# An xDeepFM forward pass on one core: rows laid out through DRAM, eight of thirteen row pairs copied by DMA, layer 1 in plain fp32

## The chip, the core and the metric

The kernel runs on one core of one Trainium2 chip. The metric is the device time of one execution in microseconds. The engines are TensorE (PE), VectorE (DVE), ScalarE (ACT), GpSimd (POOL) and SyncE (SP, which only issues DMAs here).

## The reference

512 samples with 26 sparse features each; every feature has a table of 1250 rows of 32 numbers, and 13 dense inputs stand beside them. What costs time:

```
emb = tables[feat_idx, sparse]                     # 512 x 26 x 32
x0 = xk = emb
for w, bb in ((conv1_w, conv1_b), (conv2_w, conv2_b)):          # the two CIN layers
    hp = einsum('bhd,bmd->bhmd', xk, x0).reshape(-1, h * M, E)  # all products of rows
    xn = sigmoid(einsum('oi,bid->bod', w, hp) + bb[None, :, None])   # 128 outputs
    xk = xn[:, :64];  res.append(xn[:, 64:])
cin_out = concatenate(res, axis=1).sum(-1) @ cin_w + cin_b
h1 = tanh([emb, dense] @ W1 + b1); h2 = tanh(h1 @ W2 + b2); h3 = tanh(h2 @ W3 + b3)   # 845-1024-512-256
out = linear + cin_out + h3 @ deep_w + deep_b + bias
```

Layer 1 has 26 x 26 products (351 different ones, as it is symmetric), layer 2 has 64 x 26. Only the second half of layer 2's outputs is needed.

## The kernel before, in words

**Tiling.** The batch is cut into 16 pairs of 32 samples (`NPAIR`), a pair into two halves c of 16 samples. Half a pair is 16 x 32 = 512 columns (`CH`), so a tile of both halves is 128 partitions by 1024 columns.

**Rows.** For each pair POOL gathers the table rows (`gather`, L287 to L299: 7 indirect DMAs) into `emb`, with the sample in the partition. SP then lays them out (`lay_out`, L252; `lay_out_half`, L230 to L239) with 10 small SBUF to SBUF DMAs into `raw`: the feature in the partition, 26 of them in partitions 0 to 25 for c = 0 and 64 to 89 for c = 1, and (sample, element) in the columns. ACT rounds `raw` into `x` (`x_high`, L489) and DVE writes the rest, raw minus rounded, 32 partitions further down (`x_low`, L595), so that a selection matrix over 58 partitions rebuilds full fp32 in one fp32r matmul.

**Layer 1.** `sums_of` (L358) lets PE add row pairs by a selection matrix, in three tiles u of 117 pairs. ACT squares them twice (L508 and L509: plain and rounded), POOL (DVE for the first ones) takes the difference `sq_lo`. `layer1` (L369) makes nine fp32r matmuls per half: high weights by high squares, low by high, high by low, for three u. ACT's `sigmoid` (L511) then makes `xk` (64 rows, written twice, to partitions 0 and 64) and `res1`.

**Layer 2.** Thirteen tiles t (`T2`): tile t pairs `xk` with features 2t and 2t+1. `spread_tile` (L384) broadcasts these two feature rows over 64 partitions each, by matmul into a PSUM ring of three slots, DVE multiplies them by `xk` into `prod` (L668), and `main` (L396) makes four fp32 matmul records per tile, 128 x 64 for each half, into `conv`. The sums tiles share the three ring slots with the spread tiles (`enter`, `freed_by`).

**Order.** Each engine has its program written out by hand. PE works in groups of two tiles (`GROUPS`, seven groups): first the spread tiles of the next group, then the sums of a later pair where `SUMS_IN` says so, then `main` of this group's tiles, then half a layer 1 of the next pair where `L1_IN` says so. In DVE's order of products, `X_LOW_AT`, `TURN_AT` and `FOLD1_AT` say after which tile t the other work comes. ACT's order per pair i (L554 to L568) is `sigmoid2(i-1)`, the squares of pair i+1, `x_high(i+2)`, the sigmoids of i+1, and squares of i+2. SP's order is `lay_out(i+3)` and the load of one weight piece.

**Deep part.** W1, W2, W3 are loaded in pieces and split by POOL into high and low parts (`split_piece`, L311). Behind the last pair PE runs the three deep layers at three fp32r matmuls per product (L463).

Of the kernel before, what the change touches and what calls it, by code (L numbers as in the profile page):

```python
# [5 lines left out]
F32 = mybir.dt.float32  # L6
# [28 lines left out]
WP = 1024  # L35
DENSE_AT = 96
RX = 3
SQR = 4
GSEM = 4
RING = 3  # L40
RP = 4
SUMS_IN = ({1: (1, 0), 2: (1, 1), 3: (1, 2)},
# [3 lines left out]
L1_IN = ({4: 0, 5: 1}, {3: 0, 4: 1}, {2: 0, 3: 1}, {2: 0, 3: 1})  # L46
X_LOW_AT, TURN_AT, FOLD1_AT, LOW_AT = (12, 11, 7, 7), (9, 9, 9, 9), (5, 5, 7, 7), 7
WARM = 60
PIECE_AT = 8
# [4 lines left out]
W1A_AT = IND_AT + 3 * PB  # L54
# [6 lines left out]
def build(nc, idx, table, dense_t, const, w2, mlp1, mlp2, mlp3, sel2, out):  # L61
    with ExitStack() as ctx:
# [23 lines left out]
        ind_sb = const_sb[:, IND_AT:W1A_AT].rearrange("p (k b) -> p k b", b=PB)  # L86
# [5 lines left out]
        lin = sb("lin", [P, NPAIR, 2])  # L92
# [87 lines left out]
        def piece(k):  # L180

            if k < K1:
                n = P if k < K1 - 1 else K1_LAST
                return (wpiece[k % 2][0:n, :], mlp1[k * P:k * P + n, :], m1_hi[0:n, k, :], m1_lo[0:n, k, :])
            if k < PIECES - 1:
                j = 2 * (k - K1)
                return (wpiece[k % 2][:, :].rearrange("p (k n) -> p k n", k=2),
                        mlp2[j * P:(j + 2) * P, :].rearrange("(k p) n -> p k n", p=P),
                        m2_hi[:, j:j + 2, :], m2_lo[:, j:j + 2, :])
            return (wpiece[k % 2][:, :].rearrange("p (k n) -> p k n", k=K3),  # L190
                    mlp3.rearrange("(k p) n -> p k n", p=P), m3_hi[:, :, :], m3_lo[:, :, :])

        GROUPS = [(2 * g, 2 * g + 1) for g in range(T2 // 2)] + [(T2 - 1,)]
        slot_of, freed_by = {}, {}

        def sums_in(i, g):

            ahead, u = SUMS_IN[min(i, 3)].get(g, (0, 0))
            return (i + ahead, u) if ahead and i + ahead < NPAIR else None
# [9 lines left out]
        for t in GROUPS[0]:  # L209
            enter(("spread", t))  # L210
        for i in range(NPAIR):
            for g in range(len(GROUPS)):
                ahead = [T2 * i + t for t in GROUPS[g + 1]] if g + 1 < len(GROUPS) else \
                    [T2 * (i + 1) + t for t in GROUPS[0]]
                for r in ahead:
                    if r < NTILE:
                        enter(("spread", r))
                if sums_in(i, g):
                    enter(("sums",) + sums_in(i, g))
# [9 lines left out]

        def lay_out_half(eng, i, c):  # L230

            s, at = i % RX, HALF * c
            for g in range(NG):
                eng.dma_start(raw[s][at + g * GM:at + (g + 1) * GM, :], emb[:, i, 1 + NG * c + g, 0:E])\  # L234
                   .then_inc(raw_in[s], 16)
            for q in range(ML):
                n = q * 2 * CB + c * CB
                eng.dma_start(raw[s][at + NG * GM + q:at + NG * GM + q + 1, :],  # L238
                              emb[n:n + CB, i, 0, 0:E]).then_inc(raw_in[s], 16)  # L239
# [5 lines left out]
        def _(sp):  # L245
# [6 lines left out]
            def lay_out(i):  # L252

                s = i % RX
# [5 lines left out]
                for c in range(2 if i else 1):  # L260
                    lay_out_half(sp, i, c)
# [5 lines left out]
            for i in range(RX):  # L267
                lay_out(i)
# [3 lines left out]
            for i in range(NPAIR):  # L272
                if i + RX < NPAIR:
                    lay_out(i + RX)
                if 0 <= i - PIECE_AT + 2 < K1:
                    load_piece(i - PIECE_AT + 2)
            for k in range(K1, PIECES):
                load_piece(k)
# [522 lines left out]
```

## Time and profile before

| | us |
|---|---|
| time of the runs | 473.8 median of 3 (472.45 to 473.81) |
| the profiled execution's own time | 473.61 |
| its span | 471.8, at a mean granted clock of 0.978 |
| pairs 0 to 15 end | at 67.0 (pair 0) to 398.5 (pair 15) |
| deep layers and the end | 398.9 to 471.8 |

Busy, of the span: PE 94%, DVE 68%, POOL 58%, ACT 42%. DMA moved 12.04 MB, 26 GB/s in the mean. The busy share of an engine says how much it works, not whether it sets the end: that is read in the chain of waits. The clock is the one that TensorE was granted, 1.00 being 2.4 GHz and 0.50 being 1.2 GHz.

### The profile page before, as it was taken

What the parts mean: (1) busy time and instruction counts of PE and PEld (TensorE: products, weight loads), DVE (VectorE), ACT (ScalarE), POOL (GpSimd) and SP (SyncE); (2) the same over time, 40 slices, a digit from 0 to 9 for tenths busy, and PEclk for the clock granted to TensorE, in tenths of its full rate; (3) what the DMA queues carried; (4) which work ended last, traced back from release to release, by engine and by line L of the source; (5) the groups of instructions that cost most, each with busy time, mean ns of one, the idle gap of its engine ahead of it and who ended that gap; (6) DMA issues with size and microseconds to landing.
All of it is one profiled execution on the core that took longest, in us unless ns stands there. A gap on an engine that the chain in (4) does not pass through costs nothing.

```text
span 471.8 us, 5582 instructions
## 1 busy us (share of the span) xinstructions
PE 443.0 (94%) x2006; PEld 209.7 (44%) x2006; DVE 322.3 (68%) x351; ACT 199.7 (42%) x346; POOL 273.4 (58%) x238
## 2 busy tenths in 40 slices
PE   3574989999999999999999999999999999999998
PEld 3541334343434342434333434334343423888685
DVE  4137757787787888787969797978798687442111
ACT  3063354736464645546363635353546340111111
POOL 6343658685747566666687869686854444930000
PEclk9858899999999999999999999999999999999999
DMA  5100100100000000011102121202110100300000
GB/s 180 14 13 10 15 15 13 15 10 12 9 11 11 10 10 10 11 54 14 51 13 52 15 52 17 50 15 51 26 60 0 46 0 1 124 9 2 0 1 0
DMA packets 21945, 12.04 MB, mean 26 GB/s; under 512 B 17206, under 2 KB 19638, under 8 KB 21918
## 3 DMA queue, kind: packets, MB, share of 16 engines
q1 hardware_dynamic: 17862, 9.87, 7.7%
q0 software_dynamic: 3584, 1.76, 3.2%
q8 instruction: 16, 0.26, 0.2%
q10 hardware_dynamic: 472, 0.05, 0.1%
q14 instruction: 11, 0.09, 0.1%
HBM read 9.96 MB, written 0.00 MB: 21 GB/s over the span
## 4 chain that ended last, share of the span: by engine, by line
PE 77%; DVE 8%; issue 7%; POOL 3%; DMA 3%; SPq 1%; ACTq 1%; ACT 0%; DVEq 0%
PE conv L402 34%; PE conv L380 15%; PE ring L392 10%; DVE prod L668 8%; PE conv L463 7%; PE ring L463 7%; PE ring L365 3%; POOL emb L296 3%; DMA raw<-emb 1%; DMA emb<-in_table,rows 1%; SPq L234 1%; ACTq L234 1%; DMA idx_sb<-in_idx 0%; PE conv L482 0%; SPq L238 0%
## 5 line engine op out<-in xcount | busy, mean ns | idle before, releaser
L668 DVE TENSOR_TENSOR prod<-ring,xk 128x1024 f32<-128x1024 f32 x208 | 242.7, 1217 | 72.2 <-PE ring L392 65.7
L402 PE MATMUL conv<-prod,w_sb 128*64 128x512 f32 x832 | 205.1, 611 | 0.1
L308 POOL TENSOR_TENSOR sq_lo<-sq,sq_hi 117x512 fp32r<-117x512 f32 x88 | 110.5, 1288 | 71.1 <-ACT sq_hi L509 67.9
L296 POOL DMA_INDIRECT emb<-in_table,rows x112 | 110.3, 985 | 52.5 <-issue 29.4
L402 PEld LDWEIGHTS conv<-prod,w_sb 128*64 128x64 f32 x832 | 49.8, 136 | 93.9 <-issue 82.6
L519 ACT ACTIVATE xk<-conv,const_sb 64x512 f32<-64x512 f32 x64 | 43.7, 683 | 107.1 <-PE conv L380 106.3
L392 PE MATMUL ring<-x,sel_sb 58*128 58x512 f32 x416 | 80.8, 456 | 6.2 <-DVE prod L668 3.6
L508 ACT ACTIVATE sq<-ring 117x512 f32<-117x512 f32 x96 | 58.9, 614 | 54.2 <-PE ring L365 53.9
L392 PEld LDWEIGHTS ring<-x,sel_sb 58*128 58x128 f32 x416 | 33.1, 186 | 85.6 <-issue 41.0
L509 ACT ACTIVATE sq_hi<-ring 117x512 fp32r<-117x512 f32 x96 | 59.5, 620 | 0.0
L380 PE MATMUL conv<-sq_hi,w_hi 117*128 117x512 f32 x96 | 42.2, 439 | 0.0
L380 PE MATMUL conv<-sq_hi,w_lo 117*128 117x512 f32 x96 | 38.9, 405 | 0.0
L380 PE MATMUL conv<-sq_lo,w_hi 117*128 117x512 f32 x96 | 38.5, 401 | 0.0
L600 DVE TENSOR_TENSOR x<-raw,x 26x512 fp32r<-26x512 f32 x32 | 23.9, 748 | 14.7 <-ACT x L496 13.8
L365 PE MATMUL ring<-x,sel_sb 58*117 58x512 f32 x96 | 21.3, 447 | 12.9 <-DVE prod L668 7.8
L380 PEld LDWEIGHTS conv<-sq_hi,w_hi 117*128 117x128 f32 x96 | 18.6, 194 | 28.0 <-issue 12.6
L316 POOL TENSOR_TENSOR m_lo<-wpiece,m_hi 128x1024 fp32r<-128x1024 f32 (+1 forms) x12 | 29.8, 2487 | 1.0
L521 ACT ACTIVATE res<-conv,const_sb 64x512 f32<-64x512 f32 x32 | 21.9, 684 | 0.8
L699 DVE CAST h_hi<-hf 128x512 fp32r<-128x512 f32 x8 | 5.6, 705 | 24.3 <-ACT hf L588 24.3
L529 ACT ACTIVATE res<-conv,const_sb 128x512 f32<-128x512 f32 x16 | 11.0, 689 | 26.2 <-PE conv L402 26.2
L380 PEld LDWEIGHTS conv<-sq_lo,w_hi 117*128 117x128 f32 x96 | 18.6, 194 | 4.5
L380 PEld LDWEIGHTS conv<-sq_hi,w_lo 117*128 117x128 f32 x96 | 18.6, 194 | 3.0
(78 smaller groups left out, 307.1 us busy)
## 6 DMA issues: line engine op xcount, KB each, us to landing
wpiece<-in_mlp SPq DMA_DIRECT2D x11, 512.0 KB, 3.6
emb<-in_table,rows POOLq DMA_INDIRECT x112, 2.4
raw<-emb SPq DMA_DIRECT2D x93, 16.0 KB
raw<-emb SPq DMA_DIRECT2D x62, 2.0 KB
sel_f<-in_sel SPq DMA_DIRECT2D x1, 832.0 KB, 6.1
const_sb<-in_const SPq DMA_DIRECT2D x1, 658.0 KB, 4.5
w_sb<-in_w SPq DMA_DIRECT2D x1, 416.0 KB, 6.6
wpiece<-in_mlp SPq DMA_DIRECT2D x1, 308.0 KB
```

The costliest lines, as they stand in the source:

```text
L296: pool.indirect_dma_start(out=emb[0:n, i, j, :], out_offset=None, in_=table, in_offset=bass.IndirectOffsetOnAxis(ap=rows[0:n, i, j:j + 1], ...
L308: nc.gpsimd.tensor_tensor(sq_lo[0:UK, u, c, :], sq[0:UK, s % SQR, :], sq_hi[0:UK, u, c, :].bitcast(F32), ALU.subtract).then_inc(lo_done, 1)
L316: nc.gpsimd.tensor_tensor(lo, src, hi.bitcast(F32), ALU.subtract).then_inc(piece_lo, 1)
L365: mm = nc.tensor.matmul(sums_bank(i, u)[0:UK, c, :], sel1_sb[at:at + XK, u, :], x[i % RX][at:at + XK, :], start=True, stop=True)
L380: mm = nc.tensor.matmul(l1_bank(i, c)[:, :], w[:, u, :], s[0:UK, u, c, :], start=(u == 0 and k == 0), stop=(u == UT - 1 and k == 2))
L392: mm = nc.tensor.matmul(spread_bank(r)[:, c, :], sel2_sb[at:at + XK, t, :], x[i % RX][at:at + XK, :], start=True, stop=True)
L402: mm = nc.tensor.matmul(conv[i % 2][c * HALF:(c + 1) * HALF, :], w2_sb[:, t, :], prod[r % RP][:, c, :], start=(t == 0), stop=(t == T2 - 1))
L463: mm = nc.tensor.matmul(MLP_BANKS[n % 2], w[0:r, k, mt * P:(mt + 1) * P], h[0:r, k, :], start=(k == 0 and j == 0), stop=(k == kt - 1 and j ...
L508: nc.scalar.activation(sq[0:UK, s % SQR, :], sums_bank(i, u)[0:UK, c, :], ACT.Square)
L509: nc.scalar.activation(sq_hi[0:UK, u, c, :], sums_bank(i, u)[0:UK, c, :], ACT.Square).then_inc(hi_done, 1)
L519: nc.scalar.activation(xk[i % 2][q * HALF:(q + 1) * HALF, c, :], bank[0:HALF, :], ACT.Sigmoid, bias=small_sb[0:HALF, C_CB1:C_CB1 + 1]).the ...
L668: nc.vector.tensor_tensor(prod[r % RP][:, :, :].rearrange("p c n -> p (c n)"), spread_bank(r)[:, :, :].rearrange("p c n -> p (c n)"), xk[i ...
```

## The change

What it does:

- **Rows.** The gathers take 4 indirect DMAs per pair instead of 7. SP writes the gathered rows into a DRAM buffer `laid` (26 rows of 1024 numbers per pair, 2 DMAs in `lay_out`), and reads them back into `raw` with 2 DMAs (`fetch`).
- **Copies.** For 8 of the 13 tiles (`COPIED`) the broadcast by matmul falls away. SP reads `laid` with `copy`: two DMAs per tile, each of one 4 KB row of DRAM into 64 partitions, into a ring of `RC` = 5 tiles. DVE multiplies such a tile by `xk` in place, and `main` reads it there. Five tiles (0, 1, 5, 6, 10) go through PSUM as before, with `prod` cut to 3.
- **Groups.** PE works in three groups, (0 to 4), (5 to 9), (10 to 12); `SUMS_IN`, `L1_IN`, `X_LOW_AT`, `FOLD1_AT` are new.
- **Layer 1 in plain fp32.** One square per tile and half, no difference, three fp32 matmuls per half instead of nine fp32r ones.
- **Weight pieces.** Half as large (512 columns), 24 instead of 12. The 14 of W1 are split by ACT (`piece_high`) and DVE (`piece_low`) in pairs 1 to 14; POOL keeps the last ten behind the pairs. During the pairs POOL only gathers.

```diff
-RP = 4
-SUMS_IN = ({1: (1, 0), 2: (1, 1), 3: (1, 2)},
...
-X_LOW_AT, TURN_AT, FOLD1_AT, LOW_AT = (12, 11, 7, 7), (9, 9, 9, 9), (5, 5, 7, 7), 7
+RP = 3
+COPIED = (2, 3, 4, 7, 8, 9, 11, 12)
+SPREAD = tuple(t for t in range(T2) if t not in COPIED)
+NC, NS = len(COPIED), len(SPREAD)
+RC = 5
+LAY_AT = 3
+GROUPS = ((0, 1, 2, 3, 4), (5, 6, 7, 8, 9), (10, 11, 12))
+SUMS_IN = ({1: ((1, 0), (1, 1)), 2: ((1, 2),)},
+           {0: ((1, 0),), 1: ((1, 1), (1, 2)), 2: ((2, 0),)},
+           {0: ((1, 1),), 1: ((1, 2), (2, 0)), 2: ((2, 1),)},
+           {0: ((1, 2),), 1: ((2, 0),), 2: ((2, 1),)})
+L1_IN = ({2: (0, 1)}, {1: (0,), 2: (1,)}, {1: (0,), 2: (1,)}, {0: (0,), 1: (1,)})
+X_LOW_AT, TURN_AT, FOLD1_AT, PIECE_AT = (12, 11, 4, 3), (9, 9, 9, 9), (5, 5, 7, 7), 11
...
             def lay_out(i):
                 sp.wait_ge(rows_in[i % GSEM], ROWS * (i // GSEM + 1))
+                sp.dma_start(laid[i, 0:NG * GM, :].rearrange("(j m) (b e) -> (m b) j e", m=GM, e=E),
+                             emb[:, i, 0:NG, 0:E]).then_inc(laid_in[i % RX], 16)
+                sp.dma_start(laid[i, NG * GM:M, :].rearrange("m (b e) -> (m b) e", e=E),
+                             emb[0:ML * PB, i, NG, 0:E]).then_inc(laid_in[i % RX], 16)
+            def fetch(i):
+                sp.wait_ge(laid_in[i % RX], LAID * (i // RX + 1))
                 if i < RX:
                     sp.wait_ge(raw_zero, i + 1)
                 else:
                     sp.wait_ge(x_lo_done, 2 * (i - RX + 1))
+                for c in range(2):
+                    sp.dma_start(raw[i % RX][HALF * c:HALF * c + M, :], laid[i, :, c * CH:(c + 1) * CH])\
+                      .then_inc(raw_in[i % RX], 16)
+            def copy(n):
+                r = tile_of_copy(n)
+                i, t = r // T2, r % T2
+                if n >= RC:
+                    sp.wait_ge(main_done, tile_of_copy(n - RC) + 1)
+                sp.wait_ge(laid_in[i % RX], LAID * (i // RX + 1))
+                for k in range(2):
+                    sp.dma_start(copied[n % RC][HALF * k:HALF * (k + 1), :, :].rearrange("p c n -> p (c n)"),
+                                 laid[i, 2 * t + k, :].partition_broadcast(HALF)).then_inc(copy_in[n % RC], 16)
...
             for i in range(NPAIR):
+                if i < KW:
+                    load_piece(i)
+                for k in range(NC):
+                    n = NC * i + RC + k
+                    if n < NC * NPAIR:
+                        copy(n)
+                    if i == 0 and k == 1:
+                        lay_out(2)
+                        fetch(2)
+                    if k == (NC - 1 if i < 2 else LAY_AT) and i + RX < NPAIR:
+                        lay_out(i + RX)
                 if i + RX < NPAIR:
+                    fetch(i + RX)
...
                 for u in range(UT):
+                    pe.wait_ge(sq_done, 2 * (UT * i + u) + c + 1)
+                    mm = nc.tensor.matmul(l1_bank(i, c)[:, :], w1_sb[:, u, :], sq[i % 2][0:UK, u, c, :],
+                                          start=(u == 0), stop=(u == UT - 1))
...
+                    if t in COPIED:
+                        dve.wait_ge(copy_in[n % RC], 32 * (n // RC + 1))
+                        left = copied[n % RC]
+                    else:
+                        dve.wait_ge(spread_done, n + 1)
+                        if n >= RP:
+                            dve.wait_ge(main_done, tile_of_spread(n - RP) + 1)
+                        left = spread_bank(r)
```

## Rows read from the trace of the kernel before

**Rows 1.** The page's first part: busy us, share of the span, instructions

```profile
PE 443.0 (94%) x2006; PEld 209.7 (44%) x2006; DVE 322.3 (68%) x351; ACT 199.7 (42%) x346; POOL 273.4 (58%) x238
```

**Rows 2.** Groups by line: busy us, mean ns of one, then idle before and releasers

```profile
L668 DVE TENSOR_TENSOR prod<-ring,xk 128x1024 f32<-128x1024 f32 x208 | 242.7, 1217 | 72.2 <-PE ring L392 65.7 <-ACT xk L519 6.4
```

**Rows 3.** Windows, one pair: length, busy per engine, clock, DMA share, GB/s

```profile
249.17:271.60 22.43, 22.16 (x104) 8.87 (x102) 18.16 (x20) 11.38 (x20) 17.73 (x16) 1.00 0.17 34
```

**Rows 4.** Chain of waits in that pair: start, us, what (a few pieces)

```profile
254.59 1.87 PE conv L402 x8
...
261.27 2.30 PE conv L380 x9
263.57 0.66 PE ring L392 x4
264.23 0.23 PE ring L365 x2
```

**Rows 5.** Timeline at the end: a plain fp32 matmul, four records of 512 columns

```profile
467.62 1.88 PE L482 MATMUL conv<-h,const_sb 128*1 128x512 f32 x4
```

**Rows 6.** Timeline of ACT: sigmoid of layer 2, ends of pairs 3, 13 and 15

```profile
135.95 0.69 ACT L529 ACTIVATE res<-conv,const_sb 128x512 f32<-128x512 f32 x1 [0.81 <-PE conv L402]
...
360.31 0.69 ACT L529 ACTIVATE res<-conv,const_sb 128x512 f32<-128x512 f32 x1 [0.81 <-PE conv L402]
...
398.51 0.69 ACT L529 ACTIVATE res<-conv,const_sb 128x512 f32<-128x512 f32 x1 [11.93 <-PE conv L402]
```

**Rows 7.** Chain of waits in the first 46 us (the fourth gather, last landing, layout)

```profile
9.16 0.95 POOL emb L296
...
12.91 2.33 DMA emb<-in_table,rows
...
18.49 1.83 DMA raw<-emb
```

**Rows 8.** Timeline of ACT and DVE, first pair

```profile
20.35 0.63 ACT L496 ACTIVATE x<-raw 96x512 fp32r<-96x512 f32 x1 [10.98 <-DMA raw<-emb]
23.34 0.60 ACT L508 ACTIVATE sq<-ring 117x512 f32<-117x512 f32 x1 [2.36 <-PE ring L365]
23.83 0.59 ACT L509 ACTIVATE sq_hi<-ring 117x512 fp32r<-117x512 f32 x1
...
35.00 1.39 ACT L519 ACTIVATE xk<-conv,const_sb 64x512 f32<-64x512 f32 x2 [0.45 <-PE conv L380]
...
36.49 3.49 DVE L668 TENSOR_TENSOR prod<-ring,xk 128x1024 f32<-128x1024 f32 x3 [6.44 <-ACT xk L519]
```

**Rows 9.** Bulk DMA: an issue, landing of pieces, windows (length, clock, DMA share, GB/s)

```profile
227.86 0.58 SPq L250 DMA_DIRECT2D wpiece<-in_mlp  x1
...
DMA to landing us min/median/max: 3.5/3.6/4.5
...
341.00:343.00 2.00, 1.00 0.42 152
229.00:231.00 2.00, 1.00 0.76 260
3.00:7.00 4.00, 1.00 1.00 394
```

**Rows 10.** Windows of PE (busy, granted clock, DMA share, GB/s) and its timeline

```profile
40.90:43.60 2.70, 0.00 (x0) 1.00 0.04 3
43.60:50.20 6.60, 5.62 (x16) 0.50 0.12 13
...
44.58 0.78 PE L365 MATMUL ring<-x,sel_sb 58*117 58x512 f32 x2 [3.80 <-DVE prod L668]
```

**Rows 11.** One tile's instructions (min, median, max ns), and timeline of POOL in pair 15

```profile
L600 DVE TENSOR_TENSOR x<-raw,x x32: 681/682/2776, 21.0 to 347.2; 26x512 fp32r<-26x512 f32 x32
...
383.54 8.80 POOL L338 TENSOR_TENSOR xt_lo<-xt,xt_hi 128x512 fp32r<-128x512 f32 x7 [12.14 <-ACT xt_hi L576]
```

More of the change, by code:

```diff
@@ L58, with build @@
 CONST = SEL1_AT + NPR
-def build(nc, idx, table, dense_t, const, w2, mlp1, mlp2, mlp3, sel2, out):
+def build(nc, idx, table, dense_t, const, w2, mlp1, mlp2, mlp3, sel2, laid, out):
     with ExitStack() as ctx:
@@ L180, in piece @@
         def piece(k):
[L182 to L189, printed above, removed]
@@ L199, in sums_in, with spreads_in, spreads_up_to @@
-            return (i + ahead, u) if ahead and i + ahead < NPAIR else None
+            return [(i + ahead, u) for ahead, u in SUMS_IN[min(i, 3)].get(g, ()) if i + ahead < NPAIR]
+        def spreads_in(i, g):
+            if g + 1 < len(GROUPS):
+                return [T2 * i + t for t in GROUPS[g + 1] if t in SPREAD]
+            return [T2 * (i + 1) + t for t in GROUPS[0] if t in SPREAD and i + 1 < NPAIR]
+        def spreads_up_to(r):
+            return NS * (r // T2) + SPREAD.index(r % T2) + 1
@@ L208, in build @@
             enter(("sums", 0, u))
-        for t in GROUPS[0]:
-            enter(("spread", t))
+        for r in spreads_in(-1, len(GROUPS) - 1):
+            enter(("spread", r))
         for i in range(NPAIR):
             for g in range(len(GROUPS)):
[L213 to L219, printed above, removed]
+                for r in spreads_in(i, g):
+                    enter(("spread", r))
+                for j, u in sums_in(i, g):
+                    enter(("sums", j, u))
         def l1_bank(i, c):
@@ L266, in _ @@
             sp.dma_start(w2_sb[:, :, :], w2).then_inc(w2_in, 16)
-            for i in range(RX):
-                lay_out(i)
+            lay_out(0)
+            fetch(0)
+            for n in range(RC):
+                copy(n)
+            lay_out(1)
+            fetch(1)
             sp.wait_ge(zeroed, 1)
@@ L320, in _ @@
             pool.wait_ge(idx_step, 5)
-            for i in range(RX):
+            for i in range(NPAIR):
                 gather(i)
-            for i in range(NPAIR):
-                if i + 1 < NPAIR:
-                    for u in range((1, 0, 1)[i] if i < 3 else 2, UT):
-                        low(i + 1, u)
-                if i + RX < NPAIR:
-                    gather(i + RX)
-                if 0 <= i - PIECE_AT < K1:
-                    split_piece(i - PIECE_AT)
-                if i and i + 2 < NPAIR:
-                    for u in range(1 if i == 1 else 2):
-                        low(i + 2, u)
             for k in range(K1):
@@ L341, in _ @@
             pool.wait_ge(lin_done, 1)
-            for k in range(K1, PIECES):
+            for k in range(KW, PIECES):
                 split_piece(k)
@@ L530, in sigmoid2, with piece_high @@
                                      bias=small_sb[:, C_CB2:C_CB2 + 1]).then_inc(l2_read, 1)
+            def piece_high(k):
+                src, _, hi, _ = piece(k)
+                act.wait_ge(piece_in[k % 2], 16 * (k // 2 + 1))
+                nc.scalar.activation(hi, src, ACT.Copy).then_inc(piece_hi, 1)
             act.wait_ge(zeroed, 1)
@@ L558, in _ @@
                         squares(i + 1, u)
+                        if (i, u) == (2, 1):
+                            x_high(i + 2)
                 if i == 1:
                     sigmoid(2, 0)
-                if i + 2 < NPAIR:
+                if i != 2 and i + 2 < NPAIR:
                     x_high(i + 2)
+                if i <= KW:
+                    piece_high(i - 1)
                 if i + 1 < NPAIR:
@@ L565, in _ @@
                         sigmoid(i + 1, c)
+                        if (i, c) == (2, 0):
+                            squares(4, 0)
                 if i + 2 < NPAIR:
-                    for u in range(1 if i == 1 else 2):
+                    for u in range(1 if i == 2 else 0, 1 if i == 1 else 2):
                         squares(i + 2, u)
             act.wait_ge(l1_done, 2 * NPAIR)
-            act.wait_ge(lo_done, 2 * UT * NPAIR)
             act.wait_ge(turned, 2 * NPAIR)
@@ L796 @@
             for k, v in arrays.items()}
+    laid = nc.dram_tensor("laid", (NPAIR, M, 2 * CH), F32, kind="Internal").ap()
     out = nc.dram_tensor("out_row", (B,), F32, kind="ExternalOutput").ap()
-    build(nc, out=out, **args)
+    build(nc, laid=laid, out=out, **args)
     r = run_bass_kernel_spmd(nc, [{f"in_{k}": v for k, v in arrays.items()}], core_ids=[0])
```

207 lines of the change are left out of this document (82 added, 125 removed), and 3 rows, old and new, of the table SUMS_IN.

## The prediction

> **What bounds the kernel now.** I read the page's busy shares first: PE 94%, DVE 68%, POOL 58%, ACT 42% [rows 1]. That names a candidate. The window of one steady pair confirms it: 22.16 of 22.43 us are PE, at the full clock, while DVE has 18.16 [rows 3]. The chain of waits in that pair shows what fills it: two tiles of `main` take 1.87, half a layer 1 takes 2.30, two spread tiles with the change of matmul kind before and after 0.66, a sums tile 0.23 [rows 4]. So PE sets the pace, and a DVE product (1.217 alone [rows 2], 1.14 back to back, as three take 3.49 [rows 8]) waits 65.7 us in all for the ring. Pair 3 ends at about 135.75, pair 13 at 360.1, pair 15 at 398.35 (each sigmoid of layer 2 starts 0.2 behind) [rows 6]: 22.44 per pair in between. All sums below go by the profiled execution, 473.6, which stands 0.2 under the median of 473.8.
>
> **PE's work per pair.** Spread tiles: 8 of 13 go, and four of seven group changes. Per pair before, 13 x 0.935 + 2 x 2.30 + spreads and sums of some 5.7 = 22.4. After: `main` stays 12.15. Five spreads and three sums cost 8 x 0.23 + 3 x 0.2 for the changes = 2.4, that is 0.90, 0.66 and 0.90 in the three groups. Layer 1 does not get cheaper: a plain fp32 matmul of 512 columns is two records of about 0.43 each, since four take 1.88 less a tail of 0.17 [rows 5]; three per half are 6 x 0.43 to 0.45 = 2.65, against 2.30. PE's own floor is 12.15 + 5.3 + 2.4 = 19.9 per pair.
>
> **DVE.** 18.16 [rows 3] plus 0.7 for `piece_low` = 18.9. I take a product from SBUF at the price of one from PSUM; the row of x_low, an SBUF by SBUF operation of 512 columns at 682 ns [rows 11], would give 0.15 + 2 x 0.53 = 1.22, the same. ACT loses half its squares and gains 0.6 of `piece_high`; it is not near 19.9. The squares' difference on POOL hid beside PE and frees nothing on the path.
>
> **The loop through xk.** Layer 1's second half now ends in group 1, and the next pair's products wait for the sigmoids: 0.2 + 1.39 [rows 8] = 1.65; five products and x_low, 5.8 + 1.4 (two operations of 0.68 [rows 11]); `main` of tile 4, 0.93; first half 2.65; group change 0.66; `main` of 5 to 9, 4.67; second half 2.65. Sum 20.4. With nothing else in the way a pair would take 20.4, 2.0 less than now.
>
> **The loop through fetch, which I think decides.** In pair i (from 3 on) DVE does x_low(i+2) behind product 3. That needs x_high(i+2), which needs `raw`, fetched by SP at the end of its iteration i-1. In front of this fetch stands the copy of tile 8 of pair i, which waits for `main` of tile 12 of pair i-1: the end of that pair. Call this end zero.
> Issues: a bulk DMA takes SP 0.58, 0.63 with the step to the next [rows 9]. The copy of tile 7 (freed by tile 11) issues at -0.7, that of tile 8 at 0.5 to 1.8, the fetch at 1.8 and 2.4. The last small layout DMA landed 1.83 from its issue [rows 7], so 4.25 is the earliest with 0.58 issues. If an issue costs 0.43 it is 3.5.
> Transfer: the copies of tiles 7 and 8 are 1 MB in the same queue ahead of the fetch. No row shows a load into only 64 partitions. Bounds: the 128-partition loads ran at 394 GB/s when the queue was full, the one 77-partition piece at 152 against 260 for a full piece seen alone [rows 9]. 64 partitions are nearer to 77 than to 128, so there will be a loss; I take half of 394, 200 GB/s, or 1.31 per 256 KB transfer (0.66 and 1.7 at the ends). A piece's bytes moved from about 1.1 behind its issue and it landed 0.5 behind the last of them. So: first byte at 0.4, four transfers 5.25, the fetch's 0.1 MB 0.25, 0.5: `raw` lands at 6.4.
> The Trainium skill, page SBUF — State Buffer, section "Door 1: The DMA port swizzle", says that partitions 0 to 63 reach only 8 of 16 ports, 196 GB/s against 328 for 128 partitions at 1 MiB, and that two DMAs to the two halves gain only 6%. By it a copy takes 2.6 us. No run here shows it yet; it speaks against a change that sends 67 MB to SBUF in halves of 64 partitions.
> From there: x_high 0.05 + 0.64, x_low 0.05 + 1.40, product 4 1.20; then 0.93 + 2.65 + 0.66 + 4.67 + 2.65 + 0.90 + 2.80 (tiles 10 to 12) = 15.27. Period = landing + 18.6 = 25.0.
> Clock: PE stands still from 4.65 (`main` of tile 3) to 9.75, 5.1 us per pair. In the trace before, PE stood still for 3.8 us ahead of 44.58; the granted clock was 0.50, the 1.2 GHz level, from 43.6 to 50.2, with 5.62 us busy in it [rows 10], so work worth 2.8 was lost. I take 2.5. Period 27.5.
> Ten pairs (4 to 13): 10 x (27.5 - 22.44) = +50.6. With the ends of my bounds: landing 3.5 gives 22.1 (-3), 152 GB/s lands at 8.0 and gives 26.6 + 2.5 = 29.1 (+67).
>
> **The first pairs.** The fourth gather starts at 9.16 and would land 2.33 later, 11.5, instead of 15.24 for the seventh [rows 7]. Writing to `laid` (two issues and a landing of 2.3, bounds 1.8 and 3.5) and the fetch bring `raw` at 17.7 instead of 20.3. Six squares at 0.48 instead of twelve [rows 8] end at 23.7; the first half of layer 1 runs at the low clock (5.1), the second not (2.65), sigmoids 1.6: first product at 32.6 instead of 36.49 [rows 8]. Pair 0: 18.4 of DVE, `main` 0.9, then both halves of layer 1 uncovered and the sigmoids around x_high(2), 6.5 = 25.8. Pairs 1 and 2: DVE 19, `main` 0.9, half a layer 1 2.65, 1.65, stalls for x_low of 0.6 and 1.5: 24.8 and 25.7. Pair 3 meets its `raw` in time: 22.6. It ends at 131.5, against 135.75: -4.2 (bounds -8 and +1, as the clock may fall in the uncovered stretches).
>
> **The end.** Pair 14 has no x_low: 19.5. Pair 15 is DVE's 16.9 behind xk: 19. POOL's seven differences, 8.8 us in pair 15 [rows 11], now lie beside products with two SBUF operands; x_low, also such, once took 2776 ns instead of 682 beside POOL's work [rows 11]. I add 3 (0 to 7). 41.5 against 38.25: +3.3. The deep part keeps its matmuls: 0. What hides POOL's last ten pieces is the deep layer 1; each costs a load that lands in 3.6 [rows 9] and a split, shared by two buffers. Without that cover it would be up to 5.
>
> **Sum.** 473.6 - 4.2 + 50.6 + 3.3 = 523.
>
> **Rivals.**
> - *Half rate, clock kept.* Same loop, but PE is granted 1.00: period 25.0, 473.6 - 0.9 + 25.6 = 498. For it: the trace has one such fall in the pairs, and a standstill that comes in every pair may be met otherwise. Against it: 5.1 us is more than the 3.8 that was enough [rows 10]. 0.14.
> - *Full rate.* The copies move as fast as 128-partition loads; the issues decide, landing 3.5 to 4.25, period 22.1 to 22.9, 469 to 477; with an occasional fall of the clock up to 490. The busy engines of the 77-partition piece moved as much each as those of a full one (152 at a share of 0.42, 260 at 0.76 [rows 9]), which speaks for it. 0.22, of which a quarter is faster than before.
> - *The fetch is no bound (other side).* If `raw` lands within 1.8 us of the pair's end, or another order of events hides it, the xk loop sets the pace: 20.4, so 473.6 - 0.9 - 20.4 = 452. It decides below a landing of 1.8; the break-even of the whole is 3.9. For it: PE loses 2.5 us of work and ACT has slack. Against it: two waits and four issues in one queue. 0.22.
> - *The copies bind by volume.* 4.2 MB per pair at 152 GB/s are 27.6 us, to which the fetch, the layout, the gathers and a weight piece add over 1 us: 29 per pair, 473.6 - 0.9 + 66 = 539. The DMA engines would never rest. 0.10.
>
> **Chances.** The forecast has 0.32, the volume case 0.10, clock kept 0.14, full rate 0.22, fetch no bound 0.22. A change of 0.3% (1.4 us) is about what this kernel's times can tell. Faster: 0.22 + 0.06 = 0.28; same 0.04; slower 0.68. The range leaves out a tenth on each side: 454 to 542. The likeliest case's own range is 507 to 540.
>
> **What would show it.** Step by step in the changed profile: DVE's wait at x_low for ACT's x, some 4 us per pair, and ACT's x_high waiting for DMA raw; PE idle near 5 us per pair ahead of `main` of tile 4, with a clock of 0.5 behind it; half a layer 1 at 2.65; a copy's 256 KB transfers spaced 1.3 us; first product near 32.6; pair 3 ending near 131. Wrong: a DMA share near 1 only half the time with copies at 0.7 each (full rate), or pairs of 20 to 21 us with PE busy throughout (no bound).

## The result, and the profile after

| | before | after |
|---|---|---|
| median of the runs, us | 473.5 | 594.1 (591.4 to 598.2, 4 runs) |
| ratio | 1 | 1.2555 [1.2510, 1.2599] |
| span of the profiled execution | 471.8 | 596.3, mean granted clock 0.88 |

The kernel before ran at 473.5 beside it. Slower by 120.6 us where 49.5 were forecast: the right side, but outside the range of 454 to 542. The profiled execution of the changed kernel is the slowest of its four, 4 us above the median, so the rows below add up to 124.5 and not to 120.6. Of the kernel in "The first pairs again" four of six runs were over 1.5% longer than its fastest, and its time and ratio are those of the other two. The first part of the changed kernel's page, beside [rows 1], shows TensorE with more busy time although it has 354 fewer matmul records, and idle for a fifth of the span:

```profile
PE 462.9 (78%) x1652; PEld 186.8 (31%) x1652; DVE 317.8 (53%) x356; ACT 162.7 (27%) x264; POOL 151.0 (25%) x146
```

The sigmoid of layer 2 marks the ends of pairs 3, 13 and 15, as in [rows 6]:

```profile
162.58 0.69 ACT L550 ACTIVATE res<-conv,const_sb 128x512 f32<-128x512 f32 x1 [3.34 <-PE conv L430]
...
483.44 0.69 ACT L550 ACTIVATE res<-conv,const_sb 128x512 f32<-128x512 f32 x1 [3.34 <-PE conv L430]
...
522.44 0.69 ACT L550 ACTIVATE res<-conv,const_sb 128x512 f32<-128x512 f32 x1 [15.54 <-PE conv L430]
```

From these rows and the spans, term by term (us):

| stretch | before | after | moved | forecast |
|---|---|---|---|---|
| start to the end of pair 3 | 135.95 | 162.58 | +26.6 | -4.2 |
| pairs 4 to 13 | 224.36 | 320.86 | +96.5 | +50.6 |
| pairs 14 and 15 | 38.20 | 39.00 | +0.8 | +3.3 |
| deep layers, end | 73.3 | 73.9 | +0.6 | 0 |

A steady pair takes 32.09 instead of 22.44. The page's list of waits (us in total, times, longest) names the loop that was forecast, fetch to x_high to x_low to product to `main` of tile 4, and one wait that was not, that of the sums (L394) for ACT's squares:

```profile
DVE x L628 <- ACT x L520: 118.1, 14, 10.9
...
PE conv L430 <- DVE copied L694: 62.2, 15, 7.6
ACT x L520 <- DMA raw<-laid: 59.6, 12, 10.5
...
PE ring L394 <- ACT sq L529: 31.7, 12, 2.6
```

The chain of waits (start, us, what) through one steady pair, from the end of the pair before at 322.60 (`...` marks pieces left out):

```profile
318.16 4.44 PE conv L430 x12
322.60 0.02 issue
322.62 0.45 SPq L297
...
323.11 0.60 SPq L297
...
323.80 0.50 SPq L286
...
324.34 5.09 DMA raw<-laid
...
329.46 0.64 ACT x L520
...
330.83 0.68 DVE x L628
...
331.55 1.24 DVE copied L694
...
332.83 1.98 PE conv L430 x4
334.80 3.44 PE conv L408 x6
338.24 0.44 PE ring L420 x2
338.68 0.23 PE ring L394 x2
338.91 4.44 PE conv L430 x20
343.35 2.79 PE conv L408 x6
...
347.58 0.68 ACT res L542
...
348.29 1.09 ACT sq L529 x2
...
349.43 0.50 PE ring L394 x2
```

Read it downwards: the copy's issue waits for the pair's last `main`, and the fetch stands behind it in SyncE's queue. Beside this chain TensorE still has spreads, sums and `main` of tiles 0 to 3 to do, up to 327.06; then it stands for 5.77 us, as its timeline shows:

```profile
332.83 1.98 PE L430 MATMUL conv<-copied,w_sb 128*64 128x512 f32 x4 [5.77 <-DVE copied L694]
```

Behind it comes a cold stretch, one in which the granted clock has fallen (0.70 from 332.83 to 338.24): 1.98 for `main` of tile 4 and 3.44 for half a layer 1, against 1.08 and 2.79 where the clock is full. At 346.14 it leaves TensorE a second time, for ACT's sigmoids and squares, and comes back at 349.43; the twelve records behind that gap take 4.44, which is the first line (the same place one pair earlier); the granted clock is 0.64 from 349.9 to 354.4. The windows of that pair and of its copies (length, busy per engine, clock, DMA share, GB/s), beside [rows 3]:

```profile
322.60:354.30 31.70, 23.29 (x82) 7.56 (x82) 18.41 (x20) 9.21 (x15) 6.83 (x8) 0.84 0.65 151
322.60:329.30 6.70, 4.46 (x22) 1.45 (x22) 0.00 (x0) 1.78 (x3) 0.99 (x2) 1.00 1.03 233
```

While copies run the DMA engines are full (share 1.03) at 233 GB/s, not 394 as for 128 partitions in [rows 9]. Over the whole pair their share is 0.65, so volume does not bind.

### The profile page after: what moved, and what is told of

Its sections match the earlier page's. It is cut to its first block, busy times and chain, and to the rows that moved or that the text cites. A ratio compares the mean times of both kernels' runs of the same rounds, so it can differ in the third digit from the quotient of the medians.

```text
span 596.3 us, 4837 instructions
## 1 busy us (share of the span) xinstructions
PE 462.9 (78%) x1652; PEld 186.8 (31%) x1652; DVE 317.8 (53%) x356; ACT 162.7 (27%) x264; POOL 151.0 (25%) x146
## 4 chain that ended last, share of the span: by engine, by line
PE 58%; issue 10%; DMA 9%; DVE 9%; SPq 6%; ACT 6%; POOL 1%; DVEq 0%
PE conv L430 26%; PE conv L408 16%; DMA raw<-laid 8%; PE conv L487 6%; PE ring L487 5%; SPq L297 5%; DVE copied L694 5%; PE ring L420 2%; DVE prod L694 2%; PE ring L394 2%; ACT sq L529 2%; DVE x L628 2%; ACT xk L540 2%; ACT x L520 1%; ACT res L542 1%
## 5 line engine op out<-in xcount | busy, mean ns | idle before, releaser
L430 PE MATMUL conv<-copied,w_sb 128*64 128x512 f32 x512 | 146.5, 699 | 67.0 <-DVE copied L694 62.2
L694 DVE TENSOR_TENSOR copied<-copied,xk 128x1024 f32<-128x1024 f32 x128 | 156.2, 1244 | 10.6 <-DMA copied<-laid 10.2
L694 DVE TENSOR_TENSOR prod<-ring,xk 128x1024 f32<-128x1024 f32 x80 | 94.9, 1215 | 84.7 <-ACT xk L540 78.8
L408 PE MATMUL conv<-sq,w_sb 117*128 117x512 f32 x192 | 110.0, 718 | 2.2 <-ACT res L542 2.2
L430 PE MATMUL conv<-prod,w_sb 128*64 128x512 f32 x320 | 90.7, 683 | 0.7 <-DVE prod L694 0.7
L430 PEld LDWEIGHTS conv<-copied,w_sb 128*64 128x64 f32 x512 | 39.6, 156 | 159.3 <-DVE copied L694 84.1
L628 DVE TENSOR_TENSOR x<-raw,x 26x512 fp32r<-26x512 f32 x32 | 21.8, 682 | 118.7 <-ACT x L520 118.1
L408 PEld LDWEIGHTS conv<-sq,w_sb 117*128 117x128 f32 x192 | 41.4, 231 | 78.8 <-issue 75.4
L394 PE MATMUL ring<-x,sel_sb 58*117 58x512 f32 x96 | 21.2, 453 | 41.4 <-ACT sq L529 31.7
L420 PE MATMUL ring<-x,sel_sb 58*128 58x512 f32 x160 | 34.6, 483 | 12.7 <-DVE prod L694 8.9
L367 POOL TENSOR_TENSOR xt_lo<-xt,xt_hi 128x512 fp32r<-128x512 f32 (+1 forms) x7 | 15.4, 2248 | 83.5 <-ACT xt_hi L604 83.5
L430 PEld LDWEIGHTS conv<-prod,w_sb 128*64 128x64 f32 x320 | 20.1, 147 | 38.9 <-issue 34.6
L420 PEld LDWEIGHTS ring<-x,sel_sb 58*128 58x128 f32 x160 | 13.5, 192 | 56.1 <-issue 31.8
L520 ACT ACTIVATE x<-raw 96x512 fp32r<-96x512 f32 x16 | 10.1, 630 | 59.6 <-DMA raw<-laid 59.6
L394 PEld LDWEIGHTS ring<-x,sel_sb 58*117 58x117 f32 x96 | 9.1, 188 | 48.5 <-ACT sq L529 36.9
```

Source lines behind the costliest of these rows:

```text
L394: mm = nc.tensor.matmul(sums_bank(i, u)[0:UK, c, :], sel1_sb[at:at + XK, u, :], x[i % RX][at:at + XK, :], start=True, stop=True)
L408: mm = nc.tensor.matmul(l1_bank(i, c)[:, :], w1_sb[:, u, :], sq[i % 2][0:UK, u, c, :], start=(u == 0), stop=(u == UT - 1))
L420: mm = nc.tensor.matmul(spread_bank(r)[:, c, :], sel2_sb[at:at + XK, t, :], x[i % RX][at:at + XK, :], start=True, stop=True)
L430: mm = nc.tensor.matmul(conv[i % 2][c * HALF:(c + 1) * HALF, :], w2_sb[:, t, :], prod_of(r)[:, c, :], start=(t == 0), stop=(t == T2 - 1))
L628: nc.vector.tensor_tensor(x[i % RX][at + XLO:at + XK, :], raw[i % RX][at:at + M, :], x[i % RX][at:at + M, :].bitcast(F32), ALU.subtract).t ...
L694: nc.vector.tensor_tensor(prod_of(r)[:, :, :].rearrange("p c n -> p (c n)"), left[:, :, :].rearrange("p c n -> p (c n)"), xk[i % 2][:, :, ...
```

## The experiments

Each kernel is the changed one with the edit shown, unless it says otherwise. "Steady pair" is the mean of pairs 4 to 13. In the edits `...` marks lines left out, and copies are counted from 0. The kernel before took 471.4 to 472.9 beside them.

**The fetch moved forward.** Behind copy 5 instead of behind copy 7 of its pair.

```
+FETCH_AT = 5
...
-                if i + RX < NPAIR:
-                    fetch(i + RX)
+                    if k == (NC - 1 if i < 2 else FETCH_AT) and i + RX < NPAIR:
+                        fetch(i + RX)
```

> SP fetches raw(i+3) behind the copy that tile 9 frees instead of behind the one that tile 12 frees. Theory (each steady pair of 32.1 us is a loop through the late fetch, with a ring-slot wait of 3 and a fallen clock on top): DVE's wait for x_high, 118 us in all, falls under 20; what is left per pair is PE's own work with the slot wait, 0.9 + 4.7 + 2.8 + 0.7 + 4.7 + 2.8 + 3.8 + 2.8 = 23.1, so the whole is 594 - 10 x 9 = 504. Rival (the copies bind by their volume): the queue only shifts the wait to the copies, at most a third of that comes back, 560 or more, and DVE then waits for copied tiles.

Measured 524.4 us, 1.112 [1.106, 1.118]; steady pair 24.86. Moving the fetch gives 7.2 us per pair back. ScalarE's wait for `raw` fell from 59.6 to 11.1 us in all, but VectorE's wait for x_high only from 118.1 to 66.0, where under 20 was expected. The pair did not get as short as expected, because x_high(i+2) stands in ACT's queue behind the squares of the next pair's last sums. In the chain of this kernel, the end of the pair's tiles is followed by spreads, sums, squares and only then x_high, though its rows are there:

```profile
306.01 2.73 PE conv L431 x12
308.74 0.66 PE ring L421 x4
309.40 0.26 PE ring L395 x2
...
310.17 0.59 ACT sq L530
310.76 0.52 ACT x L521
...
312.02 0.68 DVE x L629
...
312.73 1.24 DVE copied L695
...
314.01 1.08 PE conv L431 x4
```

**The ring slot alone.** squares(i+2, 0) go between the two sigmoids, as the kernel does for pair 4 only, so that the slot they hold is free when group 2 begins.

```
-                        if (i, c) == (2, 0):
-                            squares(4, 0)
+                        if i >= 2 and c == 0 and i + 2 < NPAIR:
+                            squares(i + 2, 0)
-                    for u in range(1 if i == 2 else 0, 1 if i == 1 else 2):
+                    for u in range(1 if i >= 2 else 0, 1 if i == 1 else 2):
```

> ACT squares sums(i+2,0) before the second sigmoid of pair i+1 instead of behind it; nothing else. Theory: sums(i+2,1) no longer waits in PE for that ring slot, its 31.7 us of waiting (12 times) go, 3 us per pair, 594 - 30 = 564, and the wait for raw stays. Rival (the slot wait lies beside the wait for raw and only moves): no change, 594.

Measured 550.7, 1.168 [1.162, 1.174]; steady pair 28.36, 3.7 less. The waits of sums for squares fell from 12 times to one. The twelve records behind them had taken 4.4 in eight of the pairs 4 to 13 and 2.8, the full-clock price, in two; now they take 2.8 in all ten:

```profile
PE ring L394 <- ACT sq L529: 2.6, 1, 2.6
```

This shows the unforecast wait, and that it took clock with it in most pairs. The wait itself was 2.6 (31.7 over 12). In the mean of pairs 4 to 13 the stretch from the end of layer 1's second half to the pair's end fell from 7.9 to 3.7, that is by 4.2; 3.7 came back, since `main` of tile 4 started 10.8 behind the pair's end instead of 10.2: the loop through fetch took the rest. Pair 3 gained as much, 22.9 instead of 27.5.

**x_low later.** Behind product 6 instead of 3, so that the wait for it holds back three products fewer.

```
-X_LOW_AT, TURN_AT, FOLD1_AT, PIECE_AT = (12, 11, 4, 3), (9, 9, 9, 9), (5, 5, 7, 7), 11
+X_LOW_AT, TURN_AT, FOLD1_AT, PIECE_AT = (12, 11, 4, 6), (9, 9, 9, 9), (5, 5, 7, 7), 11
```

> x_low of pair i+2 stands behind product 6 instead of product 3 in DVE. Theory: main of tile 4 and half a layer 1 now run while raw is on its way; the wait comes at the sums in group 1, 9 us behind the pair's end instead of 14.5 of work and cold clock, so 5.4 to 6.6 us per pair come back: 528 to 540. Rival (volume of the copies): 594 or little less, DVE waits for copied tiles instead.

Measured 518.7, 1.100 [1.093, 1.107], steady pair 24.55: better than expected. The same late fetch costs 7.5 us per pair less when `main` of tile 4 and the first half of layer 1 no longer stand behind it. In the profiled execution pair 0 also ended 6.1 sooner (66.4 instead of 72.5), though the edit leaves it alone: VectorE waited 3.4 for the copy of tile 12 instead of 5.3, TensorE stood 2.8 instead of 4.7, and both halves of layer 1 behind that took 2.84, at the full clock.

**All three.**

> The three edits together. Theory: what is left is the loop through xk (20.4), PE's own 20.1 and the DMA queue, 4.2 MB per pair at the 235 GB/s seen with the engines' share at 1.0 plus some 2 us for the rest, 20.5: 21 per steady pair, 594 - 111 = 483 with the first pairs as they are. Rival (volume): DMA share near 1.0 throughout and 24 or more per pair, 510 or more.

Measured 481.5, 1.020 [1.015, 1.025]; steady pair 21.19, alternating near 20.2 and 22.8; clock 0.95. The pairs are now shorter than before's 22.44 and the kernel is still slower, because pair 2 ends at 134.1 against 113.5. So two things were left: the first pairs and the alternation.

**What limits the copies' rate.** First the source: the copies read 64 rows of W1 in DRAM instead of one row 64 times, so `copied` holds other data.

```
-                                 laid[i, 2 * t + k, :].partition_broadcast(HALF)).then_inc(copy_in[n % RC], 16)
+                                 mlp1[HALF * k:HALF * (k + 1), :]).then_inc(copy_in[n % RC], 16)
```

> The changed kernel, but each copy reads 64 different DRAM rows of 4 KB (W1's) instead of one row 64 times, so its products are not the reference's; destination, size, count and waits are the same. Theory (the copy's rate is set by its destination of 64 partitions): no change, 594, and 215 to 245 GB/s while the engines' share is 1.0. Rival (set by the source, one row read 64 times): near the 394 GB/s of the 128-partition loads, raw lands 2.5 us sooner, 594 - 25 = 569.

Then the destination: one DMA of 128 partitions, all with the row of the first pair member, so the second half of `copied` holds the wrong row.

```
-                for k in range(2):
-                    sp.dma_start(copied[n % RC][HALF * k:HALF * (k + 1), :, :].rearrange("p c n -> p (c n)"),
-                                 laid[i, 2 * t + k, :].partition_broadcast(HALF)).then_inc(copy_in[n % RC], 16)
+                sp.dma_start(copied[n % RC][:, :, :].rearrange("p c n -> p (c n)"),
+                             laid[i, 2 * t, :].partition_broadcast(P)).then_inc(copy_in[n % RC], 32)
```

> The changed kernel, but each copy is one DMA of one DRAM row into all 128 partitions (512 KB as before) instead of two of one row each into 64, so the second feature of a pair is replaced by the first. Theory (destination): 350 to 400 GB/s while the queue is full; raw lands some 3 us sooner, of which one issue of 0.6 less per copy is a part; 540 to 565. Rival (source): 215 to 245 GB/s still, and only the saved issues show: 585 to 594.

Measured 595.3 (1.258 [1.249, 1.267]) and 583.3 (1.233 [1.222, 1.244]). Windows with the copies running, of the first kernel and of the second:

```profile
320.00:329.00 9.00, 4.60 (x24) 1.53 (x22) 1.90 (x3) 2.92 (x5) 1.08 (x2) 1.00 1.01 242
```

```profile
20.00:26.00 6.00, 4.03 (x11) 1.88 (x12) 1.36 (x2) 3.04 (x6) 4.72 (x5) 0.59 1.02 281
319.00:323.00 4.00, 0.66 (x4) 0.00 (x0) 0.18 (x1) 0.84 (x2) 0.00 (x0) 1.00 0.97 315
```

Rereading one row is not what slows them: 242 against 233. Writing all 128 partitions from one DMA gives 281 to 315, part of the way to 394; neither theory had the number, and what keeps the rest was not settled. The time hardly moves: in this kernel's chain `raw` lands 6.1 behind its issue, where it was 5.1. With one issue per copy the fetch enters the same queue earlier and waits there longer (argued, not tried). The rate is a small term of this loop.

**Layer 1 in plain fp32, alone, in the kernel before.** Three fp32r products per tile become one of fp32; GpSimd's differences of squares and their waits go.

```
...
-                    for k, (w, s) in enumerate(((w1_hi, sq_hi), (w1_lo, sq_hi), (w1_hi, sq_lo))):
-                        mm = nc.tensor.matmul(l1_bank(i, c)[:, :], w[:, u, :], s[0:UK, u, c, :],
-                                              start=(u == 0 and k == 0), stop=(u == UT - 1 and k == 2))
+                    mm = nc.tensor.matmul(l1_bank(i, c)[:, :], w1_hi[:, u, :], sq_hi[0:UK, u, c, :],
+                                          start=(u == 0), stop=(u == UT - 1))
...
```

> The kernel before with one part of the change alone: layer 1 as three plain fp32 matmuls per half, one square per tile and half, no difference. Theory: half a layer 1 takes 2.79 instead of 2.29 on a PE that sets the pace, 16 x 2 x 0.5 = +16 less about 1 at the start: 488. Rival (POOL's and ACT's freed work matters): no slower than 474.

Measured 487.6, 1.033 [1.026, 1.041], as expected. This part of the change costs about 1 us per pair by itself: two halves of 2.79 where [rows 4] had 2.30.

**SyncE's order in the first pairs, on top of all three.** In pair 0 the copy of tile 12 stood in the queue behind lay_out(2) and fetch(2); it now goes ahead of them, and lay_out(3) and fetch(3) move into pair 1.

```
-                    if i == 0 and k == 1:
+                    if i == 0 and k == 2:
                         lay_out(2)
                         fetch(2)
+                    if i == 1 and k == 1:
+                        lay_out(3)
+                        fetch(3)
-                    if k == (NC - 1 if i < 2 else LAY_AT) and i + RX < NPAIR:
+                    if k == (LAY_AT if i > 1 else NC - 1) and 1 <= i < NPAIR - RX:
                         lay_out(i + RX)
...
```

> all3 (481.5 us: the early fetch of rows, x_low behind the last product from position 6, squares of the pair after next between the sigmoids) with another order of SyncE's work in pairs 0 to 2: the copy of pair 0's tile 12 goes ahead of lay_out(2) and fetch(2), lay_out(3) and fetch(3) move from behind pair 0's last copy into pair 1. In all3 VectorE stands 5.95 us for the copy of tile 12, and ACT's x_high(2) and x_high(3) hold back the second sigmoid of pairs 1 and 2, so pair 0 ends at 71.7 and pair 1 at 105.7. Theory (the loss over the first pairs is SyncE's order, each wait sits on the path): pair 0 ends about 61, pair 2 about 118 instead of 134, and the whole 465 to 470 (ratio 0.985 to 0.995). Rival (the copies themselves, 8 tiles behind two gathers on the same queues, set these pairs): under 4 us of it come back, 478 to 482.

Measured 474.6 (10 runs), 1.0034 [0.9997, 1.0070]: between the two. Pair 0 ends at 63.3 instead of 71.7, and the 8 us are kept through pair 2 (126.1), but pairs 1 and 2 themselves stayed at 34.5 and 28.3. The theory holds for pair 0 alone.

**The gathers one pair further ahead.** Added to the last.

```
-                if i:
-                    pool.wait_ge(laid_in[(i - 1) % RX], LAID * ((i - 1) // RX + 1))
+                if i > 1:
+                    pool.wait_ge(laid_in[(i - 2) % RX], LAID * ((i - 2) // RX + 1))
```

> start_fix, and the gathers of a pair wait for the rows laid out of the pair before the previous one instead of the previous one. In all3 the steady pairs alternate (about 20.2 and 22.8), and the chain that ended last runs gathers (9 us), their landing (8.1), lay_out at 322.41, copies stopped behind it in SyncE's queue. Theory (this ring is what the alternation comes from): steady pairs go to 20.2 to 20.6, that is 6 to 10 us less than start_fix, 456 to 462 us. Rival (the copies' volume on the DMA engines is the bound: 8.4 MB per two pairs at 233 GB/s is 18 us of 20 per pair): no more than 2 us less than start_fix.

Measured 462.3, 0.981 [0.974, 0.988]: faster than the kernel before. Steady pair 20.09, no alternation. What showed the ring in all3 was its chain, which ran through POOL's gathers, their landing and SyncE's layout, with the copies queued behind it:

```profile
312.58 1.43 POOL emb L347
...
314.32 8.08 DMA emb<-in_table,rows
...
322.41 0.39 SPq L274
...
330.80 9.52 DMA copied<-laid
```

Now both limits are met at once. In 40 us of this kernel TensorE is busy for 40.00 and the DMA share is 1.00:

```profile
300.00:340.00 40.00, 40.00 (x166) 13.91 (x164) 37.63 (x42) 19.00 (x31) 0.00 (x0) 1.00 1.00 243
```

**One DMA per copied tile.** Added to the last; the source is an access pattern of two rows, each repeated 64 times, the data are the same.

```
-                for k in range(2):
-                    sp.dma_start(copied[n % RC][HALF * k:HALF * (k + 1), :, :].rearrange("p c n -> p (c n)"),
-                                 laid[i, 2 * t + k, :].partition_broadcast(HALF)).then_inc(copy_in[n % RC], 16)
+                src = bass.AP(laid.tensor, laid[i, 2 * t, :].offset, [[2 * CH, 2], [0, HALF], [1, 2 * CH]])
+                sp.dma_start(copied[n % RC][:, :, :].rearrange("p c n -> p (c n)"), src).then_inc(copy_in[n % RC], 32)
```

> gather_ahead, and each copied tile in one DMA of 128 partitions (its source row changes at partition 64) instead of two DMAs of 64 partitions. Computes the same. Theory (SyncE's issues, 0.5 to 0.6 us each, and the rate into 64 partitions delay the copies: dst128 showed 281 to 300 GB/s instead of 233): copies land 0.6 to 1.0 us sooner, the waits of VectorE for copied tiles (29.6 us in all3) halve, 3 to 8 us less than gather_ahead. Rival (copies land in time already once SyncE is not held back): within 1.5 us of gather_ahead.

Measured 1417 us, 3.00 [2.99, 3.02]. Neither theory saw this. VectorE waits 917 us for copies, and the windows show why: 60 GB/s at a DMA share of 0.15, that is 2.4 of 16 engines. It is not the one DMA per tile as such, for the one of a single row into 128 partitions ran at 281 to 315:

```profile
310.00:340.00 30.00, 11.57 (x30) 3.12 (x30) 7.90 (x8) 4.28 (x7) 0.00 (x0) 0.67 0.15 60
```

An outer dimension of 2 in the pattern and about two engines at work suggest that a DMA is divided over the engines by that dimension; that reading was not tried with another size.

**The first pairs again, on the kernel with the gathers ahead.** Pair 3's rows laid out and fetched behind pair 0's last copies, x_low(3) behind product 9.

```
-X_LOW_AT, TURN_AT, FOLD1_AT, PIECE_AT = (12, 11, 4, 6), (9, 9, 9, 9), (5, 5, 7, 7), 11
+X_LOW_AT, TURN_AT, FOLD1_AT, PIECE_AT = (12, 9, 4, 6), (9, 9, 9, 9), (5, 5, 7, 7), 11
-                    if i == 1 and k == 1:
-                        lay_out(3)
-                        fetch(3)
-                    if k == (LAY_AT if i > 1 else NC - 1) and 1 <= i < NPAIR - RX:
+                    if k == (LAY_AT if i else NC - 2) and i + RX < NPAIR:
                         lay_out(i + RX)
-                    if k == (FETCH_AT if i > 1 else NC - 1) and 1 <= i < NPAIR - RX:
+                    if k == (FETCH_AT if i else NC - 1) and i + RX < NPAIR:
                         fetch(i + RX)
```

> gather_ahead (462.3 us) with pair 3's rows laid out behind the copy of pair 0's tile 11 and fetched behind the next, pair 4's and all later ones at positions 3 and 5 of the copies, and x_low(3) behind the product of tile 9 instead of 11. In gather_ahead TensorE stands 3.61 us in pair 1 for x_low(3), whose rows were laid out at 73.4 and fetched at 78.5 us, and 0.5 clock follows (tiles 10 to 12 take 5.5 us where 2.8 is the warm price). Theory (the fetch behind SyncE's queue still sets pair 1): 3.6 + 2.7 = 6 us less in pair 1, 455 to 458, ratio 0.966. Rival (the second half of layer 1 at the end of pairs 0 to 2, which nothing covers, sets these pairs): under 1.5 us less, 461 to 463.

Measured 478.8 (478.1 and 479.5; the other four runs 486.5 to 489.1), 1.014 [1.010, 1.019], where 455 to 458 was expected. The expectation failed, and not in the place it spoke of: pair 1 took 37.3 (34.2 without the edit), steady pairs 20.12 as before, and pair 0 ended 13.6 later. Timeline rows of ACT and PE (start, us, what, idle before and releaser):

```profile
36.42 3.04 ACT L530 ACTIVATE sq<-ring 117x512 f32<-117x512 f32 x6 [15.20 <-remote]
...
37.65 1.68 PE L421 MATMUL ring<-x,sel_sb 58*128 58x512 f32 x4 [13.31 <-issue]
```

ACT and TensorE both stood from about 24 to 36 us for nothing that the profile shows; the sums that ACT needed were there at 24.3. The DMA engines were full from 20 to 32 us in the kernel without this edit too, where no such gap is, and the edited steps come later than 54 us. The cause of the gap stays open.

**SyncE's order alone, in the changed kernel.** The edit of "SyncE's order in the first pairs", without the three edits below it.

> The changed kernel (594.1 us) with nothing but SyncE's order in pairs 0 to 2 changed, as in start_fix. Theory (the order costs the changed kernel what it cost all3: pair 0's tile 12 waits for its copy, 5 us, cold clock behind it): pair 2 ends at about 127 instead of 135.1, the steady pairs stay at 32.1, the whole 585 to 588. Rival (the lateness is taken up by the ring of the fetch, which starts from the end of each pair anyway): 592 to 595.

Measured 589.1, 1.248 [1.244, 1.252]. Pair 2 ends at 126.3 instead of 135.1, the steady pair stays at 32.07. The profiled spans differ by 8.9, the medians by 5.0, less than the 6 to 9 expected. Not all of that is the order: with the order unchanged, "x_low later" and "the ring slot alone" ended pair 2 at 129.2 and 130.5, as TensorE's gap in pair 0 was 2.8 and 2.6 there and layer 1 behind it kept its clock.

## Why the prediction was right or wrong

**The sign and the loop were right.** "The loop through fetch, which I think decides": the chain goes through the very steps named, and moving the fetch or x_low out of it brought back 7.2 and 7.5 us per pair. The rival that the fetch is no bound fell, but its sum for a pair was near: with the loop dissolved a pair takes 20.09, where 20.4 was worked out. That is in part luck. The 20.4 was a loop with x_low in front of tile 4; in that kernel x_low stands behind product 6 and TensorE never rests (the window of 40.00), so what the time lies near is TensorE's own 19.9.

**The period, 27.5, was 32.09.** By the forecast's own terms, from the chain above:

| term | forecast | measured |
|---|---|---|
| `raw` lands behind the pair's end | 6.4 | 6.8 |
| to the start of `main` of tile 4 | 3.35 | 3.4 |
| `main` of 4, first half, cold | 0.93 + 2.65 + 2.5 for clock | 1.98 + 3.44 |
| group change, `main` 5 to 9, second half | 7.98 | 0.67 + 4.44 + 2.79 |
| to the first record of tiles 10 to 12 | 0.90 | 3.79 |
| tiles 10 to 12 | 2.80 | 4.44 |

The rows add to 27.5 and 31.8; this pair took 31.7. The landing's rise, the halves and the clock behind the first gap were sized within 0.3 us together. In the mean of pairs 4 to 13 the same stretches are 10.25 to the start of `main` of tile 4 (forecast 9.75), 6.0 for it and the first half (6.08), 7.9 up to the end of the second half (7.98), and 7.9 to the pair's end (3.70). The step that failed is "0.66 and 0.90 in the three groups", the price of group 2's change: it counted the records of spreads and sums and not the wait in them. Sums (i+2, 1) write the ring slot that sums (i+2, 0) hold until their squares are taken, and these squares stand in ACT behind the sigmoid of layer 1's second half. In this pair that is 2.9, and 1.6 more for the clock that falls behind it; in the mean of the ten pairs it is 2.9 and 1.3, so 4.2 of the 4.6 by which the period was missed, or 42 of 46 us. The slot experiment took these 4.2 out, 3.7 of them net. The prediction added up what TensorE issues in group 2 and did not trace who frees each slot.

**Pair 3's end, forecast -4.2, was +26.6.** The start is 1.25 of it: the first product came at 33.85, not 32.6. Here I misread the code: a pair still has seven gathers, not four (the page has x112 for 16 pairs), so the seventh still rules. The larger part is in the pairs, 38.6, 34.3, 28.3 and 27.5 against 25.8, 24.8, 25.7 and 22.6. Rows of the first product and of pair 0:

```profile
33.85 2.36 DVE L694 TENSOR_TENSOR prod<-ring,xk 128x1024 f32<-128x1024 f32 x2 [12.19 <-ACT xk L540]
...
55.28 1.23 DVE L694 TENSOR_TENSOR copied<-copied,xk 128x1024 f32<-128x1024 f32 x1 [5.26 <-DMA copied<-laid]
...
58.47 5.10 PE L408 MATMUL conv<-sq,w_sb 117*128 117x512 f32 x6
...
65.76 4.54 PE L408 MATMUL conv<-sq,w_sb 117*128 117x512 f32 x6 [2.19 <-ACT res L542]
```

In pair 0 VectorE stood 5.3 for the copy of tile 12, and layer 1 ran cold behind it. In the profiled executions changing SyncE's order took 8.8 us off the end of pair 2; but 4.6 and 5.9 went without that change where the clock did not fall, so the order by itself is some 3 to 4 and the fallen clock the rest. Pair 3's 4.9 is the ring slot again (4.6 of it came back in the slot experiment), and pair 2's 2.6 is the size of the one wait for squares that experiment left. The prediction listed SyncE's queue for the steady pairs only and took the first pairs' copies as in time; what had to be asked there was what stands ahead of each copy in the queue. Pairs 1 and 2 stayed at least 9.5 and 6.5 us longer than before's in all kernels of the experiments on the first pairs. In pair 1 of the changed kernel the chain has a wait of sums for x_low(3), 3.6, twelve records behind it at 5.3 instead of 2.8, and twenty at its start at 6.8 instead of 4.4; the attempt to shorten pair 1 failed, so this part is argued only.

**The rate.** "64 partitions are nearer to 77 than to 128": right, with 233 instead of 200 GB/s and engines busy throughout; the full-rate rival is refuted by that row, the volume rival by the share of 0.65. By the Trainium skill, page SBUF — State Buffer, section "Door 1: The DMA port swizzle", partitions 0 to 63 reach half the ports, and by its 196 for one transfer of 1 MiB the rate would be near 200, an estimate; the trace agrees in direction, and the measurement, 233, decides. The same table gives about 218 as the limit of half the ports, which 233 passes by 7%. Its 328 for 128 partitions at 1 MiB lies between the 281 to 315 of the one-DMA copy and the 394 of [rows 9]. What it can't explain is that the rate mattered so little: 20% to 35% more of it was worth 11 us of 594.

**The clock.** It fell, as forecast, behind the gap ahead of tile 4: 0.84 over the pair. "Clock kept" is refuted. Against the full-clock prices of the forecast it cost 1.8 there in the pair of the chain and 2.4 in the mean of the ten pairs, where 2.5 was taken, and 1.3 in the mean a second time, behind the gap that had not been seen.

**The end.** +0.8 where 3.3 was taken. GpSimd's seven differences beside products with two SBUF operands did slow down, to 15.4 us in all from 8.80 [rows 11]. A product with two SBUF operands took up to 2308 ns, but 1244 in the mean, and pair 15 took 19.9 where 19 and a surcharge of 3 were forecast: the surcharge was mis-sized, it was 0.9.

## What to carry to other kernels

When a transfer's issue stands in a queue behind a wait, add the loop up, then follow every other engine around the same loop: each ring slot it needs, and what the engine that frees it has queued in front. A gap of a few microseconds on TensorE can cost a second time in its clock: here an unseen wait of 2.9 brought 1.3 more in the mean, all of it from eight of ten pairs. Steady pairs can't be priced for the first ones: there the queues are in another order, and here that was a fifth of the loss. An idea that loses 25% as laid out can win 2% when the waits around it, none of them in its arithmetic, are taken out.

## What the runs showed of the hardware

- Copies from DRAM into 64 partitions each ran with all DMA engines busy at 233 GB/s where they read one row 64 times and at 242 where they read 64 rows; into 128 partitions in one DMA 281 to 315.
- A DMA whose source pattern had an outer dimension of 2 moved 60 GB/s on about 2.4 of 16 engines: a kernel of 462 us took 1417.
- TensorE standing 2.64 or 2.65 us was followed by a fallen clock in eight of ten steady pairs (twelve records 4.4 instead of 2.8) and by the full clock in two; behind 2.8 and 2.6 in pair 0 of two kernels the clock stayed full, behind 4.7 in the changed kernel it fell.
- A plain fp32 product of 512 columns with 128-column weights took 0.465 per record (2.79 for six), against 0.256 for fp32r in layer 1 (2.30 for nine).
- An instruction stream can stand for 13 us on two engines with nothing in the profile to show for it; here it came with an edit whose steps run later than 54 us, in a stretch that ended at 37.65.
